# Shifting relative-position scores with moves of two rows over eight tiles in place of four rows over four

## The reference

```python
x = x + 0.5 * ffn(layernorm(x))
x = x + attn(layernorm(x))
x = x + 0.5 * ffn(layernorm(x))
# attn, per batch and head, i and j over 2048:
AC = einsum('bhid,bhjd->bhij', q + u_bias, k)
BD = einsum('bhid,hjd->bhij', q + v_bias, rp)
BD = rel_shift(BD)          # row i is read i places further left
attn = softmax((AC + BD) * scale)
out = einsum('bhij,bhjd->bhid', attn, v)
```

## Time and profile before

| | us |
|---|---|
| median of 3 runs | 3423.48 (3422.01 to 3426.68) |
| profiled execution, its own time | 3423.38 |
| its span | 3421.6 |
| TensorE busy | 3015.8 (88%) |
| ScalarE busy | 2591.6 (76%) |
| VectorE busy | 2486.6 (73%) |
| GpSimd busy | 2404.1 (70%) |

### The profile page before, as it was taken

One profiled execution on the slowest core, in us unless ns is written; L12 is line 12 of the kernel. 1 busy time (PEld: TensorE's weight loads), 2 busy tenths in 40 slices (PEclk: granted clock), 3 DMA queues, 4 the chain that ended last, 5 costly groups with the idle time before them and its releaser, 6 DMA issues. The chain is left out here.

```text
span 3421.6 us, 112672 instructions
## 1 busy us (share of the span) xinstructions
PE 3015.8 (88%) x40768; PEld 2061.1 (60%) x40768; DVE 2486.6 (73%) x4784; ACT 2591.6 (76%) x4106; POOL 2404.1 (70%) x4104
## 2 busy tenths in 40 slices
PE   4556399999999999998999999999999999989965
PEld 2444066666666666666666666666666666666645
DVE  2555177777787878787878787877787787878866
ACT  2334388888888878787888888887888888878832
POOL 3223687777788878786878877877877887868820
PEclk8778599999999999999999999999999999999987
DMA  5232799999999999999999989999999999999951
GB/s 188 92 104 97 185 202 208 201 201 204 199 210 208 212 198 211 199 212 191 207 217 208 216 198 205 208 205 198 215 206 207 208 210 211 206 198 206 209 155 50
DMA packets 326603, 655.70 MB, mean 192 GB/s; under 512 B 191536, under 2 KB 283568, under 8 KB 292784
## 3 DMA queue, kind: packets, MB, share of 16 engines
q0 software_dynamic: 190464, 524.79, 72.4%
q1 hardware_dynamic: 135600, 123.75, 14.8%
HBM read 77.48 MB, written 46.14 MB: 36 GB/s over the span
## 5 line engine op out<-in xcount | busy, mean ns | idle before, releaser
L653 POOL DMA_DIRECT2D score<-score x3968 | 2272.5, 576 | 632.8 <-ACT score L894 568.9
L892 ACT COPY score<-pos_bank 128x512 f32<-128x512 f32 x2048 | 1087.9, 608 | 439.1 <-PE pos_bank L768 434.3
L902 ACT ACTIVATE score<-score,low 128x1024 f32<-128x1024 f32 x1024 | 1211.3, 1184 | 17.5 <-DVE low L953 11.7
L835 PE MATMUL pt_bank<-ident_sb,score 128*128 128x128 f32 x8192 | 1121.5, 278 | 29.5 <-issue 20.6
L835 PEld LDWEIGHTS pt_bank<-ident_sb,score 128*128 128x128 f32 x8192 | 954.5, 142 | 317.3 <-DVE prob_t L962 78.7
L953 DVE CUSTOM_DVE_ANT_0 score<-ac_bank,score 128x1024 f32<-128x1024 f32 x512 | 627.0, 1225 | 571.0 <-PE ac_bank L821 526.2
L962 DVE COPY prob_t<-pt_bank 128x512 f32<-128x512 f32 x1536 | 1008.6, 684 | 10.0 <-PE pt_bank L835 9.1
L953 DVE CUSTOM_DVE_ANT_0 score<-ac_bank,score,low 128x1024 f32<-128x1024 f32 x512 | 656.5, 1282 | 115.4 <-PE ac_bank L821 95.9
L768 PE MATMUL pos_bank<-pos,qv 96*32 96x512 bf16 (+15 forms) x12160 | 635.6, 318 | 80.8 <-DMA qv<-qv_parts 53.8
L849 PE MATMUL acc_bank<-prob_t,vs 128*32 128x128 f32 x16384 | 678.2, 281 | 29.8 <-issue 29.5
L821 PE MATMUL ac_bank<-ks,qu 96*128 96x512 bf16 x2048 | 628.8, 389 | 13.0 <-issue 7.1
(11 more groups left out here) (94 smaller groups left out, 935.9 us busy)
## 6 DMA issues: line engine op xcount, KB each, us to landing
score<-score POOLq DMA_DIRECT2D x3968, 129.0 KB, 6.5
pos<-pos_parts SPq DMA_DIRECT2D x96, 128.0 KB, 9.3
ks<-k_parts SPq DMA_DIRECT2D x192, 64.0 KB, 7.5
qu<-qu_parts SPq DMA_DIRECT2D x768, 16.0 KB, 7.8
qv<-qv_parts SPq DMA_DIRECT2D x576, 16.5 KB, 6.9
v_heads<-v_sb SPq DMA_DIRECT2D x8, 1024.0 KB, 7.3
vs<-v_heads SPq DMA_DIRECT2D x32, 256.0 KB, 9.0
pos_parts<-part SPq DMA_DIRECT2D x16, 384.0 KB, 2.7
```

The costliest lines, as they stand in the source:

```text
L653: pool.dma_start(pairs_of_tiles(score[s::QUAD, at:at + FT, :], 0), pairs_of_tiles(score[s::QUAD, at:at + FT, :], QUAD - 1 - s))\
L835: last = pe.matmul(PT[c % 2][:, t * P:(t + 1) * P], lhsT=score[:, slot(k), c * BANK + t * P:c * BANK + (t + 1) * P], rhs=ident_sb[:, :], i ...
L892: act.copy(score[:, at + f, c * BANK:(c + 1) * BANK], ring(m)[:, :]).then_inc(pos_out, 1)
L902: act.activation(cols, cols, ACT.Exp, bias=low[:, slot(k), NH - 1:NH], scale=-1.0)\
```

## The change

One move now takes two rows, s and s+64 (or s+32 and s+96), over two groups, four tiles to a run of 8288 elements. The 31 moves that follow the completion of an even group j take the odd quads (rows s+32 and s+96) of groups j-1 and j; those that follow an odd group take the even quads (s and s+64) of j-1 and j. The very first set holds group 0 alone, and one more set at the end holds the last group's odd quads. There are four semaphores, two for each kind of quad, and the add of a group's first tile waits for two of them.

Positions are made 14 tiles ahead, and their 17 pieces lie on four bodies as 4, 4, 4 and 5 (`MADE_OF`, by the tile that is made). Group J is complete at the end of body 4J-11. The fold goes to k % 4 = 2, the finish to 3. `take` waits tile by tile for the ring's place. SyncE's loads of qv move with the positions.

```diff
-            POS_AHEAD, AC_AHEAD = 11, 2
+            POS_AHEAD, AC_AHEAD = 14, 2
...
-            MADE_AT = (range(0), range(0, 6), range(6, 12), range(12, ITEMS))
-            FOLD_AT = MADE_AT[1].stop
+            MADE_OF = (range(0, 4), range(4, 8), range(8, 12), range(12, ITEMS))
+            FOLD_AT = MADE_OF[0].stop
...
-                return (k - FT - 1) // FT
+                return (k - FT - 2) // FT
...
-                items = MADE_AT[k % FT]
+                items = MADE_OF[(k + POS_AHEAD) % FT]
...
+                def shifted(odd, s, groups, first):
+
+                    rows = score[odd * QUAD + s::2 * QUAD, :, :].rearrange("p (g f) w -> p g (f w)", f=FT)
+                    return rows[:, groups, first:first + (FT - 1) * MWIN + L]
+
+                def move(step, j, last=False):
+
+                    if not last:
+                        wait_apart(pool, pos_out, group(step, j) * ITEMS + ITEMS)
+                    odd = 1 if last else 1 - j % 2
+                    n = (j + 1) // 2 if odd else j // 2
+                    at = j % RING
+                    if last or j == 0 and isinstance(step, int) and step == 0:
+                        groups = slice(at, at + 1)
+                    elif at == 0:
+                        groups = slice(0, RING, RING - 1)
+                    else:
+                        groups = slice(at - 1, at + 1)
                     for s in MOVE_ORDER:
                         if s < QUAD - 1:
-                            pool.dma_start(pairs_of_tiles(score[s::QUAD, at:at + FT, :], 0),
-                                           pairs_of_tiles(score[s::QUAD, at:at + FT, :], QUAD - 1 - s))\
-                                .then_inc(moved[j % RING], 16)
+                            pool.dma_start(shifted(odd, s, groups, 0), shifted(odd, s, groups, QUAD - 1 - s))\
+                                .then_inc(moved[odd][n % 2], 16)
...
+                move(STEPS, GROUPS - STEPS * (NT // FT) - 1, last=True)
...
-                    if k % FT == 0 and group_there(step, j):
+                    if k % FT == 1 and group_there(step, j):
                         positions_made(step, k + POS_AHEAD)
                         load_qv(step, j)
...
-                        dve.wait_ge(moved[k // FT % RING], use_of_ring(step, k // FT) * (16 * MOVES) + 16 * MOVES)
+                        for odd in range(2):
+                            n = (k // FT + odd) // 2
+                            dve.wait_ge(moved[odd][n % 2], rows_moved(step, n))
...
-                    if k % FT == 2 and group_there(step, (k - FT - 2) // FT):
+                    if k % FT == 3 and group_there(step, fold_no(k)):
                         finish(step, k)
```

More of the change, by code:

```diff
@@ L569, in build_program @@
             output_stored = [sem(f"output_stored{u}") for u in range(2)]
-            moved = [sem(f"moved{i}") for i in range(RING)]
+            moved = [[sem(f"moved{i}_{'even' if odd == 0 else 'odd'}") for i in range(RING // 2)] for odd in range(2)]
             pos_full, pos_out = sem("pos_full"), sem("pos_out")
@@ L748, in _ @@
                 load_ks(0, 1, range(len(K_PARTS)))
-                for j in (2, 3):
+                for j in (2, 3, 4):
                     positions_made(0, FT * (j - 1) - 1)
@@ L866, in body @@
                                 positions(step, n // FT, m)
-                        if h and k % FT == 1 and group_there(step, fold_no(k)):
+                        if h and k % FT == 2 and group_there(step, fold_no(k)):
                             fold(step, k)
@@ L870, in body @@
                             content(step, k + AC_AHEAD + h, 1 - h)
-                for j in range((POS_AHEAD + 1) // FT):
-                    for m in range(ITEMS):
-                        positions(0, j, m)
+                for n in range(POS_AHEAD):
+                    for m in MADE_OF[n % FT]:
+                        positions(0, n // FT, m)
                 for k in range(AC_AHEAD):
@@ L878, in _ @@
                 content(0, AC_AHEAD, 0)
-                tile_steps(pe, body, 2)
+                tile_steps(pe, body, 3)
             @block.scalar
@@ L885, in take @@
                 def take(step, j, m):
-                    if m == 0 and group_there(step, j - RING):
-                        act.wait_ge(turned, tile(step, (j - RING + 1) * FT) * NK)
+                    at, f, c = j % RING * FT, m // NK, m % NK
+                    if c == 0 and f < FT and group_there(step, j - RING):
+                        act.wait_ge(turned, tile(step, (j - RING) * FT + f + 1) * NK)
                     act.wait_ge(pos_full, group(step, j) * ITEMS + (m + 1))
-                    at, f, c = j % RING * FT, m // NK, m % NK
                     if m < ITEMS - 1:
@@ L934, in body @@
                             copy(step, k, NK - 1)
-                for j in range((POS_AHEAD + 1) // FT):
-                    for m in range(ITEMS):
-                        take(0, j, m)
+                for n in range(POS_AHEAD):
+                    for m in MADE_OF[n % FT]:
+                        take(0, n // FT, m)
                 for h in range(NH):
@@ L991, in _ @@
                         add(0, k, h)
-                tile_steps(dve, body, 3)
+                tile_steps(dve, body, 4)
         with ExitStack() as c3:
```

6 lines of the change are left out of this document (3 added, 3 removed).

## The result

The changed kernel takes **3660.1 us**, the median of four runs (3646.85 to 3671.1), against 3425.08 for the kernel before (3422.01 to 3432.23): a ratio of 1.0681, 95% interval 1.0632 to 1.0731. It is 6.8% slower. The profiled execution took 3670.44 us around a span of 3668.7, which is 10 us above the median, and sums over it are made against its own span: 3668.7 - 3421.6 = 247.1 us more.

The account below looks back on a forecast made before the run. TensorE, VectorE and ScalarE together were taken to set the pace, the moves hidden. Period (21.4 + 24.15)/2 + 0.5, taken as 23.2 against 22.5: +87, with 11 at the start and 5 at the end 3526 us; 8-in-10 range 3350 to 3700.

Parts of the forecast that it names:

- The cover is short by 2.75 us: First add of a group: moves need T = 24.15 us against a cover of one calm period, 21.4.
- the hole: GpSimd's issue of moves: a gap of 1.01 us after the fourth move in every second group.
- Loads on SP: nothing: SyncE's queue: same loads at the same rate, qv with one tile less of lead, cost nothing.
- Of the 1.1 us per group I keep 0.5: Stops of every engine without a releaser: 1.1 us per group before, 0.5 kept, bounds 0.3 and 1.1.
- the two chains drag each other: Group period: with groups lacking GpSimd's issue gap 0.5 cheaper, a reason to take 23.2 us instead of 23.3.
- Gain and loss cancel within 0.3, and P stays 21.4: Even positions: 1.05 us per group of waits gone, 1.3 lost on ScalarE; calm period 21.4, bounds 20.3 and 22.7.
- Start: First add, at 421.5 us before, now needs two sets of moves: 432.1, or 10.6 later.
- End: Last group needs two sets after its positions, 41.9 us against 35 to 40: 5 us put.
- issues at 576 ns: GpSimd's issue of one move: 576 ns as now, with 288 as lower bound; a sign of being right.
- the wait does not bite: Faster rival: even positions and fewer disturbances win, landing 3.2, P 20.35, 3358 us; chance 0.25.
- Landings stay long: Much slower rival: engines still at 13 GB/s, landing 9.0, period 25.9, 3861 us; chance 0.13.
- milder case: Variant of the long-landings rival: landing 6.5, disturbances 0.8, period 23.7, 3588 us.

Follow-up runs that it names:

- qu_light: The changed kernel with five of the six loads of a group's qu left out (scores not the reference's): 3639.26 us, 1.0639.
- four_rows: The changed kernel with the moves of before put back (four rows of one group), positions still 14 tiles ahead: 3640.31 us, 1.0648.
- four_rows_qu_first: The changed kernel with the four-row moves of before and SyncE's six qu loads issued ahead of the six qv loads: 3536.94 us, 1.0349.
- merged15: The changed kernel with positions 15 tiles ahead, six qu and six qv loads each made three, weight copy ahead of the pieces: 3258.16 us, 0.95.
- plain_order: The changed kernel with its moves issued row after row, so that neighbouring moves touch neighbouring rows: 5305.47 us, 1.55.

## Why the forecast of 3526 us was too low

The direction was right and the mechanism that I named was found. The size was not: +103 forecast, +235 measured (3660.1 - 3425.08). In the profiled run the groups from the first to the last took 230.5 us more, where 98 were forecast (87 and the 11 of the start), and the end 15.8 more, where 5 were. Counted over the 120 groups from the sixth on, two groups take 48.9 us where I had 46.4 (2 x 23.2). Those 2.5 us split as my sum did, into T (from an add to the add two groups on, by way of the moves) and P (a calm group); here T is counted from the last piece's copy on, and the rest is put to P:

- **"The cover is short by 2.75 us", T**: this is the term that was mis-sized most. From the last piece's copy to the add that waits it is 0.55 + 17.47 + 6.59 + 0.94 = 25.55, where I had 24.15 less the 0.4 ahead of it, 23.75: 1.8 of the 2.5. The last move's landing is 6.6 us in these sets and not 5.0: 1.6 too little, the largest error in the term. The issue took 17.47 and not 18.2 and gave 0.7 back. My sum also took something off for sets without the hole, but **the hole falls into every set that is waited for**: 17.47 there, 16.35 in the others. The last 0.94 is where qu comes after the moves; in `qu_light` it is 0.26.
- **"Loads on SP: nothing"** is the step that failed outright: a term put at nothing, because qv had not been waited for. I looked at how long before its use qv is loaded. What mattered is what the same queue issues behind it: twelve loads, in the stop shown above 18.6 us from the first issue to the end of the last, and 23.7 in the group before it (from 1465.85, 12.06 and 11.34 long), where the cover is one calm period, as for the moves. Alone it costs 176 us (`four_rows` against `four_rows_qu_light`), 103 of them by the order of two blocks. In the change it adds 21 at most to the moves' wait (3660 - 3639; 14 by the ratios, within their intervals). It is thus a small part of the missed 132 us, but it is why no single repair of the moves' side returns what the change lost.
- **"Of the 1.1 us per group I keep 0.5", and "the two chains drag each other"**: the other part of the two groups, from the add two groups back to the copy, is 22.05 us in calm and 23.36 on average, and I had 22.6. What lies in these 1.3 us is no disturbance for the most part. The first tile of a group that has waited takes 6.82 us on average, and 5.82 in the groups between (7.12 and 5.78 in `qu_light`): a stop is followed by a slower tile, 1.0 to 1.3 us, for which I had no term. What makes it slower is TensorE's clock. Windows over the first tile of two groups that had waited, behind stops of TensorE of 2.68 and 2.54 us:

```profile
1518.80:1524.50 5.70, 5.63 (x77) 3.64 (x76) 4.19 (x8) 4.47 (x7) 5.70 (x12) 1.00 0.84 223
...
1567.10:1574.30 7.20, 7.20 (x82) 4.81 (x80) 4.27 (x7) 4.37 (x7) 7.20 (x14) 0.76 0.85 223
```

In the second the clock was granted at 0.50, its lower level of 1.2 GHz, from 1567.55 to 1570.96. Of the 60 such tiles 42 have a stretch at the lower level and take 7.29 us on average; the other 18 take 5.76, like a tile that did not wait. So a wait costs more than its own length, and a sum of waits alone comes out too low. Only 0.3 per two groups are left for disturbances. I had put 1.0 there and taken 0.2 off for the two chains, so the sum of this part came near with the wrong things in it. Where nothing waits, 1.15 us per group remain with four-row moves and 0.2 with two-row moves.
- **"Gain and loss cancel within 0.3, and P stays 21.4"**: they cancel nearly. P is 21.74, 0.34 over the forecast, which in 127 groups makes 43 of the 45 us by which `four_rows_qu_light` is over the kernel before. The tile with two pieces ahead of the weight copy takes 5.82 us where its place took 4.41, and the three others 15.9 for 17.2: 1.4 lost and 1.3 won, on a P that was a little more than the 21.4 in that group. With the copy ahead of the pieces it is a gain (20.8).
- **Start**: the first add was forecast at 432.1 and came at 431.97:

```profile
431.97 1.23 DVE L965 CUSTOM_DVE_ANT_0 score<-ac_bank,score 128x1024 f32<-128x1024 f32 x1 [81.00 <-DMA score<-score]
```

- **End**: forecast 5 us later, measured 15.8 behind the last group's first move; no run takes this apart.
- Of what would show it right, the DMA share well under 0.99 (0.71), no waits for the fold's bank, waits of 1 to 5 us ahead of L965 and the alternation were seen. The period of 23.2 was not (24.3), nor were issues at 576 ns.

Of the rivals, "the wait does not bite" was wrong about the change and right about what lies under it: with one tile more of lead and qu on time the time is 3356.06, against the 3358 of that rival. Its landing of 3.2 and its P of 20.35 were not met, though (6.8 and 21.7), and the lead did it, so that the two times agree is chance. "Landings stay long" was wrong: the last move of a set lands after 6.4 us on average, not 9.0, and the share is 0.71. Its milder case, a landing of 6.5 and disturbances of 0.8, is what came, and its time was added up wrongly: (21.4 + 25.65)/2 + 0.8 is 24.3 and not 23.7, and 3423 + 1.8 x 124 + 16 is 3662 and not 3588. That this lies 2 us from the measured time is partly luck, since it has the end at 5 us and not 15.8, and no slower clock behind a wait.

## What to carry to other kernels

Where a change moves a step to another place in an engine's or a queue's order, sum what that queue issues behind it until the next need, not only the lead of the step itself: here twelve loads behind one wait were as late as the moves on which the whole argument turned. Two late transfers that end before the same instruction hide each other. Taking away one of them returned a tenth of what both cost, or less, so test them as a two by two table before calling either harmless. And a cheaper transfer is worth something only together with the lead that its new dependence asks for: the same two-row moves stand in a kernel 6.8% slower and in one 5.0% faster.

## What the runs showed of the hardware that was not expected

**A load on SyncE costs more to issue while moves are in flight.** The queue's timeline of the change, in the middle of six qu loads, behind GpSimd's set (whose issues ended at 1467.09 + 16.89 = 1483.98), and then ahead of the next set, which starts at 1494.60:

```profile
1485.50 2.39 SPq L679 DMA_DIRECT2D qu<-qu_parts  x1
...
1489.82 0.35 SPq L703 DMA_DIRECT2D vs<-v_heads  x1
...
1493.35 1.59 SPq L679 DMA_DIRECT2D qv<-qv_parts  x3
```

One issue takes 0.35 us there. Beside a set of moves six take 12.06 and 11.34, 1.9 to 2.0 us each. GpSimd's issuing is not what does it: of the loads of qu and qv between 600 and 3200 us, the 49 that begin within 2 us behind a set's last issue, while its last moves still land, take 2.4 us on average, the 89 that begin over 6 us behind it 0.37, and those beside the issuing 1.65. How much of it is the moves' data and how much SyncE's own loads in flight is not separated; with three loads for six (`merged15`) an issue beside moves takes 0.9. So SyncE's queue is slow from the start of a set on, which is right behind the last piece, where the change put all twelve.

**The issue of a move hardly depends on the number of its rows:** 547 ns with two rows over eight tiles and 576 with four over four, at equal bytes. The lower bound of half the time was far off. **The last move of a set lands sooner, though not after the 5.0 us that I took:** 9.6 us on average before, over 120 groups, and 6.4 in the change. Most sets of the earlier trace rows were below that 9.6. And the mean DMA share said nothing of transfers in each other's way, where the rate did: 0.73 at 127 GB/s in `plain_order`, 0.71 at 190 in the change. **Most stops without a releaser end when a packet of instructions has come,** as told under the lead of one tile more, **and a wait can bring TensorE's lower clock upon the tile behind it:** 7.29 us for 5.76.
